# Mixing stage, first three rounds: second sums of heads split, first turn to tokens ahead of the third sums, exp table early, scaling ahead of rank

## The chip, the cores and the metric

The kernel runs on one core of a Trainium2 chip. The metric is device time in microseconds (us) of one launch; several executions are taken and their median is compared. Five engines work side by side and meet through semaphores only: PE (TensorE, matrix products and transposes), DVE (VectorE), ACT (ScalarE), POOL (GpSimd) and SP (SyncE, here only for transfers).

## The reference, cut to what matters

Two transformer layers run over 32 sequences of 256 tokens with 128 channels. The change lies in the second half of layer 1's attention and in the routing that follows it:

```python
o = o2b_weighted_delta_rule(k, q, v, b)
o = o * rsqrt(mean(o * o, axis=-1) + 1e-06) * rms_w      # per head: 16 heads of 8 channels
x = x + ga * (o.reshape(B, L, Dm) @ Wout.T + bout)
h = _layernorm(x) * (1 + cb) + sb
x = x + gb * ffn(h)
# ffn: xn = rms_norm(h); scores = xn @ w_router.T ; the 2 best of 8 experts per token,
#      weighted by softmax(scores); the expert's rows are gathered and scattered back
```

## The kernel before, in words

The program is a row of stages (load, attention, route, experts, project, delta, mix, ffn, combine). Each stage is a block with an instruction list written out by hand for each engine, and a barrier at its end. An engine works its list strictly in order, so the place of a call in the list sets what waits behind what.

The mixing stage (`mix_phase`, tiles named `mix_...`) takes the 8192 tokens in 8 rounds of 1024 tokens (two halves of 512, called `par` 0 and 1). A round i goes through these steps; the line is that of the profile before:

- `head_squares(i)` (ACT, L2518) squares the delta stage's output; `sum_heads(i)` (PE, L2405) sums the squares of each head, 8 products of which each shows as two records in the trace; `roots` (DVE, L2645 and L166 to L178) makes the reciprocal roots by Newton steps; `round_of_roots(b)` serves the heads of round b+2, the layer norm of round b and the rms norm of round b-1 in one go.
- `narrow(i)` turns the roots (PE, L2414) and copies them out (ACT, L2525); `widen(i)` (PE, L2422) spreads them over the channels; `scale_heads(i)` (DVE, L2670, tile `mix_on`) multiplies; `project_out(i)` (PE, L2428) is the product with Wout; `add_bias(i)` (ACT, L2544, tile `mix_mixed`) and `add_mixed(i)` (DVE, L2679, tensor `xT`) add it to x.
- `back(i)` (PE, L2437) turns x to tokens; `statistics(i)` (DVE, L2687, L2691) takes mean and variance; `norm(i)` (ACT, L2535) normalizes; `channels(i)` (PE, L2443) turns back; `modulate(i)` (ACT, L2554) makes h.
- `router_and_rows(i)` (PE, L2456, L2457) makes token rows and router scores; `copy_rows(i)` (ACT, L2575) copies the rows; `choose(i)` (DVE, L2709 to L2736, ends with the tile `mix_mask`) picks two experts; `exps(i)` (ACT, L2582) and `share(i)` (DVE, L2756 to L2761) make the weights; `count(i)` (PE, L2478, L2480) and `rank(i)` (DVE, L2743 to L2752, ends with `mix_place_of`) give every token its slot in its expert's list.
- `send(i)` (POOL, L2837 to L2852) copies the slots and issues 16 indirect DMAs, one for each 128 tokens and choice, which scatter the rows to the experts' lists in memory.

Every engine loops over b from -1 to 8 and handles several rounds in one pass, for instance round b+1's projection beside round b's normalization and round b-1's choice. The expert stage (`ffn`) begins when the whole block is done, the last send included. Semaphores of interest: `heads` (sums of a round ready, one count per round), `heads_read` (those sums taken by DVE), `wide`, `newton`, `mask`.

The loop of DVE around the place that is edited reads before:

```python
                if b == 1:
                    then = choose(b - 1)
                    rank(b - 1)
                    share(b - 1, then)
                if b + 1 <= LAST:
                    scale_heads(b + 1)
```

Of the kernel before, what the change touches and what calls it, by code (L numbers as in the profile page):

```python
# [180 lines left out]
PAR = 2  # L181
# [2108 lines left out]
def mix_phase(nc, dram, g):  # L2290
# [16 lines left out]
    with Scope(nc, "mix") as s:  # L2307
# [85 lines left out]

        @block.tensor
        def _(pe):
            def sum_heads(i):
                if i > 0:
                    pe.wait_ge(c.heads_read, i)
                if i > 3:
                    pe.wait_ge(c.sums_read, i - 3)  # L2400
                for par in both:
                    pe.wait_ge(k[par].sq0, i + 1)
                    for r in range(TILES):
                        first = par * TILES + r
                        last = nc.tensor.matmul(head_sums[:, first:first + 128 - SIDE + 1:SIDE], sq[:, 0, par, 128 * r:128 * r + 128],  # L2405
                                                g.t("by_head"), start=True, stop=True)
                last.then_inc(c.heads, 1)

            def narrow(i):
                pe.wait_ge(c.newton, ROOT * (i + 1))  # L2410
                if i > 0:
                    pe.wait_ge(c.narrow_out, i)
                    pe.wait_ge(k[0].mixed, i)
                nc.tensor.transpose(narrow_ps, root_y[:, i % 2, HEAD], g.t("ident")).then_inc(c.narrow, 1)  # L2414

            def widen(i):
                pe.wait_ge(c.narrow_out, i + 1)
                for par in both:
                    if i > 0:
                        pe.wait_ge(k[par].mixed, i)  # L2420
                    for r in range(TILES):
                        last = nc.tensor.matmul(mid[par][:, 128 * r:128 * r + 128], pick[:, par * TILES + r, :], inv_t[:, :],  # L2422
                                                start=True, stop=True)
                    last.then_inc(k[par].wide, 1)

            def project_out(i, par):
                pe.wait_ge(k[par].on, i + 1)
                nc.tensor.matmul(mid[par][:, :], w_out[:, :], on[:, par, :], start=True, stop=True).then_inc(k[par].out_made, 1)  # L2428

            def back(i):  # L2430
                for par in both:
                    pe.wait_ge(k[par].x_added, i + 1)
                    if i > 0:
                        pe.wait_ge(k[par].modulated, i)
                    x = g.keptT[:, cols(i, par)]
                    for r in range(TILES):
                        last = nc.tensor.transpose(front[par][:, 128 * r:128 * r + 128], x[:, 128 * r:128 * r + 128], g.t("ident"))  # L2437
                    last.then_inc(k[par].by_token, 1)

            def channels(i, par):  # L2440
                pe.wait_ge(k[par].unit, i + 1)
                for r in range(TILES):
                    last = nc.tensor.transpose(front[par][:, 128 * r:128 * r + 128], unit[:, par, r, :], g.t("ident"))  # L2443
                last.then_inc(k[par].by_channel, 1)

            def router_and_rows(i):
                if i > 0:
                    pe.wait_ge(c.counted, i)
                for par in both:
                    pe.wait_ge(k[par].modulated, i + 1)  # L2450
                    if i > 0:
                        pe.wait_ge(k[par].rows_read, i)
                    for r in range(TILES):
                        j = par * TILES + r
                        h = h4[:, par, 128 * r:128 * r + 128]
                        nc.tensor.transpose(rowt[par][:, 128 * r:128 * r + 128], h, g.t("ident"))  # L2456
                        last = nc.tensor.matmul(logits[:, j * E1:(j + 1) * E1], h, router[:, :], start=True, stop=True)  # L2457
                    last.then_inc(k[par].turned, 1)

            def sum_rows(i):  # L2460
                if i > 0:
                    pe.wait_ge(c.sums_read, i)
                for par in both:
                    pe.wait_ge(k[par].sq2, i + 1)
                    for r in range(TILES):
                        j = par * TILES + r
                        last = nc.tensor.matmul(row_sums[:, j:j + 1], sq[:, 1, par, 128 * r:128 * r + 128],
                                                g.t("ones")[:, 0:1], start=True, stop=True)
                last.then_inc(c.row_sums, 1)

            def count(i):
                pe.wait_ge(c.route, ROUTE * i + MASKED)
                if i > 0:
                    pe.wait_ge(c.placed, i)
                    pe.wait_ge(c.counted, i)
                flat = mask[:, :, :].rearrange("p j e -> p (j e)")
                WIDTH = (SIDE + 1) * E1
                nc.tensor.matmul(counts, before[:, :], flat, start=True, stop=False)  # L2478
                for d in range(1, SIDE + 1):
                    last = nc.tensor.matmul(counts[:, d * E1:WIDTH], ones[:, :], flat[:, 0:WIDTH - d * E1],  # L2480
                                            start=False, stop=d == SIDE)
                last.then_inc(c.mask, 1)

            sum_heads(0)
            sum_heads(1)
            for b in range(-1, LAST + 2):
                if b + 1 <= LAST:
                    if b == -1:
                        pe.wait_ge(c.picks, SIDE)
                    narrow(b + 1)  # L2490
                    widen(b + 1)
                if b == -1:
                    pe.wait_ge(c.w_ready, 2)
                    pe.wait_ge(c.consts, 5)
                if b == 1:
                    count(b - 1)
                for par in both:
                    if b + 1 <= LAST:
                        project_out(b + 1, par)
                    if 0 <= b <= LAST:  # L2500
                        channels(b, par)
                if b + 3 <= LAST:
                    sum_heads(b + 3)
                if b > 1:
                    count(b - 1)
                if b + 1 <= LAST:
                    back(b + 1)
                if 0 <= b <= LAST:
                    sum_rows(b)
                    router_and_rows(b)  # L2510

        @block.scalar
        def _(act):
            def head_squares(i):
                if i > 0:
                    act.wait_ge(c.heads, i)
                for par in both:
                    nc.scalar.activation(sq[:, 0, par, :], g.vT[:, cols(i, par)], ACT.Square).then_inc(k[par].sq0, 1)  # L2518
# [65 lines left out]
            def scale_up(n):  # L2584
                if n == 0:
                    act.wait_ge(c.up_in, 16)
                some = g.w_up[:, n * (2 * E1 // PIECES):(n + 1) * (2 * E1 // PIECES), :]
                nc.scalar.activation(some, some, ACT.Copy, scale=per_channel[:, 2:3]).then_inc(c.up_scaled, 1)

            head_squares(0)  # L2590
            head_squares(1)
            head_squares(2)
            act.wait_ge(c.w_in, 48)
            for b in range(-1, LAST + 2):
                if b + 1 <= LAST:
                    narrow(b + 1)
                if 0 <= b <= LAST:
                    norm(b)
                if b >= 1:
                    copy_rows(b - 1, 0)  # L2600
                if b == 1:
                    exps(b - 1)
                for par in both:
                    if b + 1 <= LAST:
                        add_bias(b + 1, par)
                    if 0 <= b <= LAST:
                        modulate(b, par)
                if 0 <= b <= LAST:
                    square(b)
                if b >= 1:  # L2610
                    copy_rows(b - 1, 1)
                if b > 1:
                    exps(b - 1)
                if 0 <= b < PIECES:
                    scale_up(b)
                if b + 4 <= LAST:
                    head_squares(b + 4)

        @block.vector
        def _(dve):  # L2620
# [169 lines left out]
            for b in range(-1, LAST + 2):  # L2790
                if b >= 0:
                    round_of_roots(b)
                if b == 1:
                    then = choose(b - 1)
                    rank(b - 1)
                    share(b - 1, then)
                if b + 1 <= LAST:
                    scale_heads(b + 1)
                if b > 1:
                    then = choose(b - 1)  # L2800
                if b + 1 <= LAST:
# [417 lines left out]
```

## Time and profile before

| what | value |
| --- | --- |
| median of 3 runs | 2004.95 us (2000.4 to 2006.43) |
| the profiled execution | 2002.02 us, span of its instructions 2000.1 us |
| busy share of the span | PE 81%, weight loads 63%, DVE 74%, ACT 59%, POOL 55% |
| granted TensorE clock, mean | 0.904 |

The shares are means over nine stages with different limits. The mixing stage is a part of the span from about 1424 us to 1655 us. A timeline row gives start, length, engine, line, operation, tiles, count, and in square brackets how long the engine sat idle before it and what released it.

### The profile page before, as it was taken

How to read it: one execution, taken by the hardware profiler on the slowest of the kernel's cores; microseconds unless marked ns; L12 is line 12 of the kernel's file. 1: busy time of each engine (PE TensorE's matmuls, PEld its weight loads, DVE VectorE, ACT ScalarE, POOL GpSimd, SP SyncE). 2: the span in 40 equal slices, each digit the busy share in tenths (PEclk: the TensorE clock that was granted, in tenths of full speed). 3: DMA queues.
4: the chain of work that ended last, by engine and by line, in shares of the span. 5: the costliest groups of instructions: out<-in, count | busy, mean ns of one | idle time of the engine just before them, and what ended most of it. 6: DMA issues, size and time to landing. Idle time of an engine off the chain costs nothing. (4 is left out here: it accounts for less than half of the span.)

```text
span 2000.1 us, 50931 instructions
## 1 busy us (share of the span) xinstructions
PE 1612.7 (81%) x17727; PEld 1252.1 (63%) x17727; DVE 1473.4 (74%) x4099; ACT 1185.8 (59%) x2762; POOL 1096.3 (55%) x1141
## 2 busy tenths in 40 slices
PE   5599999998788695698847777777789607999994
PEld 4478888887577442344325555555568607999993
DVE  8688888887499542699979999999667624555556
ACT  4566666665279721577828888887366404565551
POOL 3278888887000286233348888888437773444440
PEclk8799999999899798799969999999766658999998
DMA  4000000000501132521000000000401112222216
GB/s 120 18 3 3 4 4 4 4 3 3 219 28 41 42 45 35 147 63 43 11 0 1 1 2 1 1 1 1 185 23 48 52 60 62 66 64 65 64 51 257
DMA packets 84954, 92.34 MB, mean 46 GB/s; under 512 B 11696, under 2 KB 69296, under 8 KB 84000
## 3 DMA queue, kind: packets, MB, share of 16 engines
q1 hardware_dynamic: 67840, 62.66, 9.9%
q0 software_dynamic: 14560, 22.24, 4.3%
q10 hardware_dynamic: 2304, 4.20, 0.5%
q8 instruction: 146, 2.39, 0.5%
q14 instruction: 104, 0.85, 0.1%
HBM read 46.14 MB, written 42.91 MB: 45 GB/s over the span
## 5 line engine op out<-in xcount | busy, mean ns | idle before, releaser
L2275 POOL TENSOR_TENSOR delta_A<-delta_A,delta_sW 128x256 f32<-128x256 f32 x256 | 193.7, 757 | 79.1 <-ACT delta_sW L2122 53.0
L2045 PE MATMUL delta_u<-delta_m,tables_sb 128*128 128x256 f32 x512 | 166.7, 407 | 82.0 <-DVE delta_m L2195 82.0
L694 ACT ACTIVATE attn_p_att<-attn_score,attn_mx 128x32 f32<-128x32 f32 (+7 forms) x512 | 150.4, 409 | 134.7 <-DVE attn_mx L756 134.7
L2895 POOL DMA_INDIRECT choice_rows<-ffn_y,ffn_xg x135 | 129.7, 961 | 170.9 <-DVE ffn_y L3002 167.4
L2122 ACT ACTIVATE delta_sW<-delta_W,tables_sb 128x256 f32<-128x256 f32 x256 | 126.7, 506 | 79.9 <-DVE delta_W L2217 76.1
L2045 PEld LDWEIGHTS delta_u<-delta_m,tables_sb 128*128 128x128 f32 x512 | 87.1, 190 | 132.7 <-DVE delta_m L2195 126.0
L2041 PE MATMUL delta_u<-delta_v_own,tables_sb 128*128 128x256 f32 x512 | 153.8, 383 | 8.7 <-DVE xnT L2182 8.7
L2852 POOL DMA_INDIRECT rows<-mix_rows,mix_slot x128 | 125.5, 980 | 47.9 <-issue 38.6
L1324 POOL DMA_INDIRECT exp_rows<-rows,slot_token x32 | 33.1, 1033 | 190.4 <-SPq L142 180.9
L2217 DVE TENSOR_TENSOR delta_W<-delta_W,delta_u 128x128 f32<-128x128 f32 x512 | 133.1, 280 | 4.5
L2204 DVE TENSOR_TENSOR delta_u<-delta_u,delta_prod 128x256 f32<-128x256 f32 x256 | 109.8, 429 | 17.8 <-PE delta_u L2045 4.2
L2286 POOL TENSOR_TENSOR delta_m<-delta_A,delta_prod 128x768 f32<-128x768 f32 x64 | 122.5, 1913 | 0.0
L2994 DVE TENSOR_TENSOR ffn_hid<-ffn_sg,ffn_val 128x384 f32<-128x384 f32 x135 | 74.8, 554 | 58.7 <-PE ffn_val L2918 58.5
L2918 PE MATMUL ffn_gate<-ffn_xgT,ffn_w_up 128*128 128x128 f32 x810 | 113.8, 277 | 0.0
L2918 PE MATMUL ffn_val<-ffn_xgT,ffn_w_up 128*128 128x128 f32 x810 | 113.7, 277 | 0.0
L2113 ACT ACTIVATE delta_v_own<-delta_v_rows,tables_sb 128x256 f32<-128x256 f32 x256 | 113.4, 495 | 0.0
L2041 PEld LDWEIGHTS delta_u<-delta_v_own,tables_sb 128*128 128x128 f32 x512 | 98.3, 192 | 23.8 <-DVE xnT L2182 10.2
L756 DVE TENSOR_REDUCE attn_mx<-attn_score 128x4 f32<-128x1024 f32 (+3 forms) x128 | 98.5, 807 | 19.6 <-PE attn_score L614 18.0
L2929 PE MATMUL ffn_y<-w_down_sb,ffn_hid 128*128 x810 | 112.4, 275 | 0.0
L2195 DVE TENSOR_TENSOR delta_m<-delta_W,delta_b 128x256 f32<-128x256 f32 x256 | 106.6, 416 | 6.9 <-DVE delta_W L2217 0.5
L2958 ACT ACTIVATE ffn_w_up<-w_up_sb 128x352 f32 x135 | 67.1, 497 | 69.6 <-PEq L146 45.3
L2918 PEld LDWEIGHTS ffn_val<-ffn_xgT,ffn_w_up 128*128 128x128 f32 x810 | 102.6, 194 | 0.0
(396 smaller groups left out, 4691.4 us busy)
## 6 DMA issues: line engine op xcount, KB each, us to landing
ffn_xg<-rows SPq DMA_DIRECT2D x135, 66.0 KB, 1.8
acc<-route_zero SPq DMA_DIRECT2D x10, 832.0 KB
comb_rows<-choice_rows SPq DMA_DIRECT2D x32, 256.0 KB, 5.3
rows<-route_rows SPq DMA_DIRECT2D x8, 640.0 KB, 3.5
load_rows<-in_x SPq DMA_DIRECT2D x16, 256.0 KB, 3.8
bT<-acc SPq DMA_DIRECT2D x16, 256.0 KB, 4.1
qT<-acc SPq DMA_DIRECT2D x16, 256.0 KB, 4.7
x_kept<-xT SPq DMA_DIRECT2D x16, 256.0 KB, 2.1
```

The lines of the kernel that those rows point to most:

```text
L694: last = nc.scalar.activation(p_att[:, gr, PAIR_OFF[n]:PAIR_OFF[n] + SLOT * (n + 1)], S[:, gr, c:c + SLOT * (n + 1)], ACT.Exp, bias=mx[:, ...
L2041: nc.tensor.matmul(corrections(h, pp % 2), g.t("same_head"), moving, start=True, stop=False)
L2045: nc.tensor.matmul(corrections(h, pp % 2), g.t("same_head"), m1[:, h].rearrange("p t d b -> p (t d b)"), start=False, stop=True).then_inc( ...
L2113: ins = nc.scalar.activation(v_own[:, group % AHEAD, d], v_rows[:, group % 2], ACT.Copy, scale=g.t("less_own")[:, d:d + 1])
L2122: nc.scalar.activation(sW[:, step % RING, :], W[:, step % RING].rearrange("p d b -> p (d b)"), ACT.Copy, scale=g.t("step")[:, bass.ds(step ...
L2217: nc.vector.tensor_tensor(W[:, t % RING, :, some(h)], W[:, (t - 1) % RING, :, some(h)], changes(h, pp % 2)[:, n], ALU.subtract).then_inc(b ...
L2275: nc.gpsimd.tensor_tensor(A[:, t % 8], A[:, (t - 1) % 8], sW[:, t % RING], ALU.add).then_inc(k.A, 1)
L2286: nc.gpsimd.tensor_tensor(m3[:, t // QUAD % 2, 0:QUAD - 1], sums, query, ALU.mult).then_inc(k.m3, 1)
L2852: nc.gpsimd.indirect_dma_start(g.rows1, bass.IndirectOffsetOnAxis(slot[:, at:at + 1], 0), rows[:, i % 2, par, j, n, :], None).then_inc(sen ...
L2895: nc.gpsimd.indirect_dma_start(g.choice_rows, bass.IndirectOffsetOnAxis(xg[:, n % RING, D:D + 1].bitcast(U32), 0), y[:, n % RING, :], None ...
L2918: last = nc.tensor.matmul(out[:, 128 * p:128 * p + 128], w_up[:, n % 4, half, 128 * p:128 * p + 128], xgT[:, n % 4, :], start=True, stop=True)
L2929: last = nc.tensor.matmul(y_ps[par][:, 0:D], hid[:, n % 4, 128 * p:128 * p + 128], g.w_down[:, bass.ds(e * P + p, 1), :].rearrange("h o d ...
```

## The change

Four edits, all in the mixing stage; no arithmetic changes and no semaphore is added.

1. `sum_heads` can do one half. Round 1's sums are cut: the half `par` 0 stays ahead of the loop, the half `par` 1 (which carries the signal `heads`) moves behind `project_out(0)`.
2. `back(0)` moves from behind `sum_heads(2)` to ahead of it.
3. On ACT `head_squares(2)` moves from ahead of the loop to the end of its first pass, and one `Exp` over a column of ones takes its place, so that the exp table is loaded there.
4. On DVE, in the pass b = 1 only, `scale_heads(2)` moves ahead of `rank(0)` and `share(0)`.

```diff
-            def sum_heads(i):
+            def sum_heads(i, some=both):
...
-                for par in both:
+                for par in some:
...
-                last.then_inc(c.heads, 1)
+                if some[-1] == PAR - 1:
+                    last.then_inc(c.heads, 1)
...
             sum_heads(0)
-            sum_heads(1)
+            sum_heads(1, both[0:1])
...
+                if b == -1:
+                    sum_heads(1, both[1:2])
+                    back(0)
                 if b + 3 <= LAST:
                     sum_heads(b + 3)
                 if b > 1:
                     count(b - 1)
-                if b + 1 <= LAST:
+                if 0 <= b < LAST:
                     back(b + 1)
...
             head_squares(1)
-            head_squares(2)
+            nc.scalar.activation(ex[:, 0, 0:1], g.t("ones")[:, 0:1], ACT.Exp)
             act.wait_ge(c.w_in, 48)
...
+                if b == -1:
+                    head_squares(2)
                 if b + 4 <= LAST:
                     head_squares(b + 4)
...
+                if b + 1 <= LAST:
+                    scale_heads(b + 1)
+                if b == 1:
                     rank(b - 1)
                     share(b - 1, then)
-                if b + 1 <= LAST:
-                    scale_heads(b + 1)
```

PE at the start of the stage, before: sums of rounds 0 and 1, then round 0's turn, widening and projection, the sums of round 2, the turn to tokens (`mix_front<-tables_sb,xT`) and round 1's turn and widening.

```order
L2405 MATMUL mix_sums<-tables_sb,mix_sq 128x16 x16
L2414 MATMUL mix_mid<-tables_sb,mix_root_y 128x128
L2422 MATMUL mix_mid<-mix_inv_t,mix_pick 128x128 x8
L2428 MATMUL mix_mid<-mix_on,mix_w_out 128x512 x2
L2405 MATMUL mix_sums<-tables_sb,mix_sq 128x16 x8
L2437 MATMUL mix_front<-tables_sb,xT 128x128 x8
L2414 MATMUL mix_mid<-tables_sb,mix_root_y 128x128
L2422 MATMUL mix_mid<-mix_inv_t,mix_pick 128x128 x8
```

The same place on PE with the change:

```order
L2405 MATMUL mix_sums<-tables_sb,mix_sq 128x16 x12
L2415 MATMUL mix_mid<-tables_sb,mix_root_y 128x128
L2423 MATMUL mix_mid<-mix_inv_t,mix_pick 128x128 x8
L2429 MATMUL mix_mid<-mix_on,mix_w_out 128x512 x2
L2405 MATMUL mix_sums<-tables_sb,mix_sq 128x16 x4
L2438 MATMUL mix_front<-tables_sb,xT 128x128 x8
L2405 MATMUL mix_sums<-tables_sb,mix_sq 128x16 x8
L2415 MATMUL mix_mid<-tables_sb,mix_root_y 128x128
```

Four products of 16 stand behind the first projection now, and the turn of x to tokens stands ahead of the third sums.

DVE in the pass b = 1, from the end of `choose(0)`, before: rank (four rows), share (three rows), then the scaling of round 2 (`mix_on`).

```order
L2736 TENSOR_TENSOR mix_mask<-mix_onehot 128x64
L2743 TENSOR_TENSOR mix_place<-mix_small,mix_base 128x64
L2746 TENSOR_TENSOR mix_base<-mix_base,mix_small 128x8
L2747 TENSOR_TENSOR mix_own<-mix_onehot,mix_place 128x128
L2752 TENSOR_REDUCE mix_place_of<-mix_own 128x16
L2756 TENSOR_REDUCE mix_total<-mix_ex 128x8
L2757 RECIPROCAL mix_total<-mix_total 128x8
L2761 TENSOR_TENSOR mix_rows<-mix_ex,mix_total 128x16
L2670 TENSOR_TENSOR mix_on<-mix_mid,xnT 128x512 x2
L2679 SCALAR_TENSOR_TENSOR xT<-mix_mixed,mod,xT 128x256 x4
```

The same place on DVE with the change:

```order
L2742 TENSOR_TENSOR mix_mask<-mix_onehot 128x64
L2676 TENSOR_TENSOR mix_on<-mix_mid,xnT 128x512 x2
L2749 TENSOR_TENSOR mix_place<-mix_small,mix_base 128x64
L2752 TENSOR_TENSOR mix_base<-mix_base,mix_small 128x8
L2753 TENSOR_TENSOR mix_own<-mix_onehot,mix_place 128x128
L2758 TENSOR_REDUCE mix_place_of<-mix_own 128x16
L2762 TENSOR_REDUCE mix_total<-mix_ex 128x8
L2763 RECIPROCAL mix_total<-mix_total 128x8
L2767 TENSOR_TENSOR mix_rows<-mix_ex,mix_total 128x16
L2685 SCALAR_TENSOR_TENSOR xT<-mix_mixed,mod,xT 128x256 x4
```

The two rows that scale round 2 moved from the end to right behind the mask.

## Rows read from the trace of the kernel before

**Rows 1.** Instructions of line L2852, the sends: ns min/median/max, first and last start.

```profile
L2852 POOL DMA_INDIRECT rows<-mix_rows,mix_slot x128: 953/960/1558, 1474.8 to 1652.9; - x128
```

**Rows 2.** Timeline of POOL: batches 0, 1 and 2 of the sends.

```profile
1474.83 1.08 POOL L2852 DMA_INDIRECT rows<-mix_rows,mix_slot  x1 [2.43 <-DVE mix_rows L2761]
...
1500.60 0.20 POOL L2840 CAST mix_slot<-mix_place_of 128x16 uint32<-128x16 f32 x1 [5.23 <-DVE mix_place_of L2752]
1502.42 0.98 POOL L2852 DMA_INDIRECT rows<-mix_rows,mix_slot  x1 [1.63 <-issue]
...
1524.24 0.97 POOL L2852 DMA_INDIRECT rows<-mix_rows,mix_slot  x1 [0.77 <-issue]
```

**Rows 3.** Timeline of PE, first three rounds.

```profile
1429.18 3.56 PE L2405 MATMUL mix_sums<-tables_sb,mix_sq 128*128 128x16 f32 x16 [0.81 <-ACT mix_sq L2518]
...
1434.15 3.79 PE L2422 MATMUL mix_mid<-mix_inv_t,mix_pick 128*128 128x128 f32 x16 [1.11 <-ACT mix_inv_t L2525]
1437.72 2.89 PE L2428 MATMUL mix_mid<-mix_on,mix_w_out 128*128 128x512 f32 x4
1442.51 3.02 PE L2405 MATMUL mix_sums<-tables_sb,mix_sq 128*128 128x16 f32 x16 [1.89 <-DVE mix_root_v L2645]
1445.37 1.95 PE L2437 MATMUL mix_front<-tables_sb,xT 128*128 128x128 f32 x8
...
1447.90 3.04 PE L2422 MATMUL mix_mid<-mix_inv_t,mix_pick 128*128 128x128 f32 x16 [0.37 <-ACT mix_inv_t L2525]
1452.99 1.70 PE L2428 MATMUL mix_mid<-mix_on,mix_w_out 128*128 128x512 f32 x2 [2.06 <-DVE mix_on L2670]
...
1457.38 1.86 PE L2405 MATMUL mix_sums<-tables_sb,mix_sq 128*128 128x16 f32 x16
...
1465.12 3.78 PE L2422 MATMUL mix_mid<-mix_inv_t,mix_pick 128*128 128x128 f32 x16 [0.37 <-ACT mix_inv_t L2525]
...
1474.62 2.08 PE L2428 MATMUL mix_mid<-mix_on,mix_w_out 128*128 128x512 f32 x2 [3.46 <-DVE mix_on L2670]
```

**Rows 4.** Timeline of ACT, first three rounds.

```profile
1428.41 1.15 ACT L2518 ACTIVATE mix_sq<-xnT 128x512 f32<-128x512 f32 x2 [3.16 <-PE mix_sums L2405]
1432.78 1.15 ACT L2518 ACTIVATE mix_sq<-xnT 128x512 f32<-128x512 f32 x2 [3.23 <-PE mix_sums L2405]
...
1471.56 1.28 ACT L2582 ACT_TABLE_LOAD   x1
1472.86 0.27 ACT L2582 ACTIVATE mix_ex<-mix_less 128x80 f32<-128x80 f32 x1
1476.73 0.69 ACT L2544 ACTIVATE mix_mixed<-mix_mid,mix_per_channel 128x512 f32<-128x512 f32 x1 [3.60 <-PE mix_mid L2428]
```

**Rows 5.** Timeline of DVE, first three rounds.

```profile
1431.04 0.29 DVE L178 SCALAR_TENSOR_TENSOR mix_root_y<-mix_root_t,mix_root_y 128x128 f32<-128x128 f32 x1
...
1440.48 1.78 DVE L2679 SCALAR_TENSOR_TENSOR xT<-mix_mixed,mod,xT 128x256 f32<-128x256 f32 x4 [1.81 <-ACT mix_mixed L2544]
...
1446.57 1.68 DVE L2687 BATCH_NORM_STATS2 mix_stats<-mix_front 128x6 f32<-128x128 f32 x8 [1.57 <-PE mix_front L2437]
...
1452.25 1.28 DVE L2670 TENSOR_TENSOR mix_on<-mix_mid,xnT 128x512 f32<-128x512 f32 x2
...
1470.38 0.22 DVE L2736 TENSOR_TENSOR mix_mask<-mix_onehot 128x64 bf16<-128x64 f32 x1
...
1473.16 0.22 DVE L2756 TENSOR_REDUCE mix_total<-mix_ex 128x8 f32<-128x64 f32 x1 [1.02 <-ACT mix_ex L2582]
...
1473.87 1.29 DVE L2670 TENSOR_TENSOR mix_on<-mix_mid,xnT 128x512 f32<-128x512 f32 x2
```

**Rows 6.** Busy time by stretch: PE, weight loads, DVE, ACT, POOL; granted clock, DMA.

```profile
1424.00:1439.80 15.80, 13.10 (x52) 11.62 (x53) 4.99 (x18) 3.73 (x8) 6.13 (x14) 0.50 0.90 359
...
1456.80:1463.70 6.90, 6.90 (x66) 6.76 (x65) 4.84 (x24) 5.03 (x8) 0.00 (x0) 0.99 0.01 4
1463.70:1480.70 17.00, 11.42 (x49) 8.46 (x47) 10.45 (x40) 9.14 (x21) 4.84 (x6) 0.50 0.05 16
```

## The prediction

> **What bounds the kernel now.** The page gives no single bound, since nine stages share the span, so I read only the stage that is edited, engine by engine in time. The first question there is which engine finishes last. The instructions of the send line come first [rows 1]: POOL issues 128 scattering transfers between 1474.8 and 1652.9 us, and the expert stage starts only when they are done. The timeline of POOL [rows 2] then shows how tightly they are packed. Batch 1 starts at 1502.42 and batch 2 at 1524.24, so 16 sends with what lies between two batches take 21.82. From batch 1's first send to the last send of all, 1652.9 - 1502.4 = 150.5 pass; six such periods (130.9) and the 15 steps inside the last batch (15/16 of a period at most, 20.5) give 151. So from batch 1 on POOL never waits for anything that matters, and whatever else gets faster there is worth nothing. Ahead of it POOL does wait: 1502.42 - 1474.83 = 27.59, that is 5.77 over a period, and the row of the slots names the wait, 5.23 for the ranks of round 1. The end of the stage therefore moves by what **batch 1's first send** moves, and by no more than the first send of batch 0 moves plus 5.77.
>
> The work that leads to that send is a chain over PE, ACT and DVE [rows 3 to 5]. It has three places where the chain stands still because of list order: the sums of round 1 ahead of round 0's turn, the sums of round 2 ahead of the turn to tokens, and the scaling of round 2 behind rank and share. The edits lie on these three.
>
> **Edit 1 and the ACT part of edit 3: start of round 0.** The roots of round 0 end at 1431.04 + 0.29 = 1431.33 [rows 5]. PE could turn them then, but is in the 16 records of round 1's sums from 1429.18 to 1432.74, and ACT, which must copy the turned roots, is in round 2's squares until 1432.78 + 1.15 = 1433.93. The widening starts at 1434.15 [rows 3, 4]. With half the sums left, PE is free at 1429.18 + 3.56/2 = 1430.96. ACT is free once the early exp is done: squares until 1428.41 + 1.15 = 1429.56, table load 1.28, one exp, below the 0.27 of the 80-column one: 1431.1. Both are in time for 1431.33. What remains is the turn and the copy. From below they take what the copy and its signals took behind the squares, 1434.15 - 1433.93 = 0.22; from above 1434.15 - 1432.74 = 1.41, from the end of the sums with ACT's delay inside. A turn is one product of the kind whose eight take 1.95, so I take 0.25 plus filling, and 0.3 for the copy with two signals, in all about 1.1: widening at 1432.4, a gain of 1.75 (bounds 1.4 to 2.6).
>
> The table load was hidden nowhere before (DVE idles 1.02 for the exp [rows 5]); now its cover is PE's half sums and the roots. Without that cover it would cost ACT up to 1431.1 - 1429.56 = 1.5 us at this place. The exp row starts at 1472.86, and the load ends at 1471.56 + 1.28 = 1472.84 [rows 4]: a load costs 1.28 and nothing behind it. The Trainium skill, page "ScalarE: Activation LUTs", section "What ACT_TABLE_LOAD costs", gives a drain of about 1380 ns on top of 1283 ns for each switch of the set. By it ACT would be free only at 1432.5, later than the turned roots, and this gain would be about 0.4 us smaller; the trace shows the 1283 ns and no drain, so I leave it out.
>
> **Edits 1 and 2: round 0's turn to tokens.** Projection of round 0 starts 1.75 earlier and ends at 1437.72 + 2.89 - 1.75 = 1438.9; if its second half, which ran behind 1439.8, gets the half clock, 0.7 later. The second half of round 1's sums, 1.8 at half clock, fills a gap in which PE waited 1.89 for DVE's roots before [rows 3]: it ends at 1440.6 to 1441.3. DVE ends adding to x at 1442.26 - 1.75 = 1440.5 (to 1441.2), and then makes the roots of round 1, which now need that second half. They took from 1442.26 to 1446.57 - 1.57 = 1445.0, so 2.8: now done at 1443.5 to 1444.2. What is late next is the turn to tokens: eight transposes of 1.95 in all start at 1440.6 to 1441.3, so the first half is there by 1442.3, before DVE needs it. So the statistics start at 1443.5 to 1444.2 instead of 1446.57, a gain of 2.4 to 3.1; with the same 5.68 behind it as before (1446.57 to 1452.25), DVE could scale round 1 at 1449.2 to 1449.9.
>
> The price is on PE and ACT: the sums of round 2 now stand behind the turn. They start at 1442.6 to 1443.2 and take 1.86 to 3.56 (full or half clock, [rows 3]): 1444.5 to 1446.8. ACT's squares of round 3 wait for that (1.15), then comes the copy for round 1: widening from 1445.9 to 1448.1 with 3.04 to 3.79: ends 1449.0 to 1451.9. Round 1's projection needs that and the scaled half: it starts between 1450.0 and 1451.7 instead of 1452.99. Gain 1.3 to 3.0; I take **2.2**, the middle, since clock there changed within the stretch before.
>
> **Edit 4: scaling ahead of rank.** `choose(0)` ends at 1470.38 + 0.22 = 1470.60; scaling began at 1473.87 [rows 5]. Nothing else holds it: the widening of round 2 ended at 1465.12 + 3.78 = 1468.90 [rows 3]. So the scaling moves 3.27 ahead of the rest of its round, and it is what both others wait for: PE idles 3.46 for it, ACT 3.60 for the projection behind it [rows 3, 4]. What moves back is rank and share, 1.29 later; but share had 1.02 of waiting for the exp with its table load, which is gone, and rank waited for the counts of PE in that time too. So batch 0's first send stays within 0.3 of where edits 1 and 2 put it, and it has room: it is batch 1 that decides. I take **3.2** for batch 1.
>
> Sum: 2.2 + 3.2 = 5.4 for batch 1's first send: 1497.0. POOL could start it one period after batch 0's first send: 1474.83 - 2.2 + 21.8 = 1494.4. So POOL still waits some 2.6 there, and the whole 5.4 reaches the end. By the bounds: 1.3 + 3.2 = 4.5 to 3.0 + 3.2 = 6.2; the limit set by POOL is 2.2 + 5.77 = 8.0.
>
> **The rivals.**
> - *The clock rises later.* The stretch from round 3's sums to the router runs at the full clock before (0.99 over 6.9 us), and the next 17 us at half [rows 6]. The same 16 records take 3.56 at half and 1.86 at full clock, so 6.9 us at full would be 13 at half. If half of the stretch falls to half clock by its new place in time, 3.1 is lost: gain 2.3. If all falls, the gain is about zero.
> - *The clock rises sooner.* PE loses two waits, 1.89 and 3.46. If this brings the full clock sooner, up to the POOL limit of 8.0 is won. For it speaks that the 17 us at half clock held PE busy only 11.42; against it that 13.10 busy of 15.80 at the stage's start were at half clock throughout [rows 6]. The Trainium skill, page "TensorE: Matmul & The Clock Gate", Part 1, says that half rate is the default and that PE's activity releases it; by that rule this case is the likelier one, and the trace agrees only in part.
> - *The chain is not what feeds batch 1.* If something outside the three places holds the ranks of round 1, the end does not move: 0 to 2 us.
> - *Slower.* Scaling now stands ahead of rank and waits for the widening of round 2, with 1470.60 - 1468.90 = 1.7 to spare. Were the widening later than that relative to `choose`, batch 0's first send would slip one for one. It decides the end only when that send comes after 1502.42 - 21.82 = 1480.6, so widening would have to be 7.5 late; for 0.3% slower some 13.5. Both hang on the same PE, whose router stands just ahead of it, so I hold little of it.
>
> **How the numbers follow.** The four executions shown run from 2000.4 to 2006.43, so 0.3%, 6 us, is about what a measurement can tell from no change. Against the profiled execution the sum gives 2002.02 - 5.4 = 1996.6, against the median 2004.95 - 5.4 = 1999.6; the mean of the four executions, 2003.45, lies between, and I predict 2003.45 - 5.4 = **1998.0**. Chances: forecast (4.5 to 6.2) 0.5; clock later, 2001, 0.2; clock sooner, 1995.5, 0.2; no effect, 2003, 0.06; slower, 2012, 0.04. The range runs from 2002.02 - 8.0 = 1994.0 to 2006.43 - 2.3 = 2004. Faster by over 0.3% means under 1998.9 against the median: the sooner clock, and three fifths of the forecast, whose gain lies just at that mark: 0.2 + 0.3 = 0.5. Within 0.3%: 0.46. Slower: 0.04.
>
> **What would show it.** Right: widening of round 0 about 1.7 after the end of half the sums; statistics of round 0 some 2.4 to 3.1 earlier; no PE wait of 3.46 ahead of round 2's projection; first sends of batch 0 about 2 and of batch 1 about 5.4 earlier, and after that the same period of 21.8 to the end. Wrong: a first send of batch 1 that moves by another amount with PE's granted clock changed in the stretch ahead of it; a wait in POOL that returns in batch 2 or later, when the rows or ranks of round 2 don't keep up; or an expert stage of another length.

## The result, and the profile after

The changed kernel takes 1992.57 us (median of 6 runs, 1991.28 to 1993.35) against 2003.07 us before (2000.4 to 2006.43, 6 runs): ratio 0.9947, 95% interval 0.9934 to 0.996, so 8 to 13 us less. Timed twice more, the ratio was 0.9955 (0.9941 to 0.9968) and 0.9943 (0.9929 to 0.9956). The forecast was 1998.0 with a range of 1994.0 to 2004.0: the direction is right, the gain is about twice the 5.4 us that were forecast, and the time lies below the range.

The profiled execution of the changed kernel took 1991.99 us, its span is 1990.0. The sends, to be set beside [rows 1]:

```profile
L2859 POOL DMA_INDIRECT rows<-mix_rows,mix_slot x128: 952/958/1556, 1468.1 to 1643.5; - x128
```

The timeline of POOL, batches 0, 1 and 2 [rows 2]:

```profile
1468.08 1.08 POOL L2859 DMA_INDIRECT rows<-mix_rows,mix_slot  x1 [1.31 <-DVE mix_rows L2767]
...
1491.15 0.20 POOL L2847 CAST mix_slot<-mix_place_of 128x16 uint32<-128x16 f32 x1 [2.58 <-DVE mix_place_of L2758]
1492.74 0.97 POOL L2859 DMA_INDIRECT rows<-mix_rows,mix_slot  x1 [1.39 <-issue]
...
1514.54 0.97 POOL L2859 DMA_INDIRECT rows<-mix_rows,mix_slot  x1 [0.77 <-issue]
```

Batches 1 and 2 still lie 21.80 apart (21.82 before), and from batch 1 to the last send pass 150.8 us (150.5 before): POOL is the bound as it was. Its first sends came 6.75 and 9.68 sooner. Of both, 1.67 is not the change: PE's first sums of the stage began at 1423.11 and not at 1424.78, and nothing ahead of them differs. Counted from the first sums, as in everything that follows, batch 0 is 5.1 sooner (45.0 for 50.05) and batch 1 is 8.0 sooner (69.6 for 77.6).

The timeline of PE at the start of the stage [rows 3]:

```profile
1423.11 3.60 PE L2405 MATMUL mix_sums<-tables_sb,mix_sq 128*128 128x16 f32 x16 [1.98 <-ACT mix_sq L2522]
1427.51 1.86 PE L2405 MATMUL mix_sums<-tables_sb,mix_sq 128*128 128x16 f32 x8 [0.81 <-ACT mix_sq L2522]
1429.80 0.45 PE L2415 MATMUL mix_mid<-tables_sb,mix_root_y 128*128 128x128 f32 x1 [0.42 <-DVE mix_root_y L178]
1430.68 3.31 PE L2423 MATMUL mix_mid<-mix_inv_t,mix_pick 128*128 128x128 f32 x16 [0.43 <-ACT mix_inv_t L2529]
1433.82 2.07 PE L2429 MATMUL mix_mid<-mix_on,mix_w_out 128*128 128x512 f32 x4
1435.73 0.96 PE L2405 MATMUL mix_sums<-tables_sb,mix_sq 128*128 128x16 f32 x8
...
1438.08 1.86 PE L2405 MATMUL mix_sums<-tables_sb,mix_sq 128*128 128x16 f32 x16
...
1441.34 3.79 PE L2423 MATMUL mix_mid<-mix_inv_t,mix_pick 128*128 128x128 f32 x16 [0.54 <-ACT mix_inv_t L2529]
1446.74 2.08 PE L2429 MATMUL mix_mid<-mix_on,mix_w_out 128*128 128x512 f32 x2 [1.61 <-DVE mix_on L2676]
...
1465.10 2.07 PE L2429 MATMUL mix_mid<-mix_on,mix_w_out 128*128 128x512 f32 x2
```

The second half of round 1's sums takes 0.96 where the first took 1.86; the sums of round 2 take 1.86 where they took 3.02 before; round 0's projection takes 2.07 and not 2.89. These are durations at full clock, as the second window below shows for the stretch that they lie in. The wait of 3.46 ahead of round 2's projection is gone, and ahead of round 1's PE waits 1.61 for DVE: PE was not what held round 1. The windows say the same (columns as in [rows 6]):

```profile
1423.10:1433.10 10.00, 8.33 (x36) 7.88 (x37) 3.30 (x12) 3.38 (x6) 5.48 (x13) 0.50 0.88 336
1433.10:1440.10 7.00, 6.53 (x43) 4.94 (x41) 5.13 (x15) 2.65 (x5) 0.00 (x0) 0.98 1.01 437
1440.10:1450.60 10.50, 8.12 (x25) 5.79 (x26) 7.54 (x32) 5.56 (x14) 0.00 (x0) 0.51 0.76 272
```

Full clock (the 2.4 GHz level) is granted from 10 us after the first sums for 7 us; before it came at 15 us [rows 6] and lasted 3.4 us, as the row of the kernel before for that stretch shows:

```profile
1439.80:1443.20 3.40, 1.51 (x8) 0.69 (x7) 2.60 (x8) 1.25 (x2) 0.00 (x0) 0.99 0.98 424
```

The timelines of ACT and DVE [rows 4, 5]:

```profile
1427.90 1.28 ACT L2596 ACT_TABLE_LOAD   x1
1429.20 0.20 ACT L2596 ACTIVATE mix_ex<-tables_sb 128x1 f32<-128x1 f32 x1
1430.35 0.28 ACT L2529 ACTIVATE mix_inv_t<-mix_mid 128x128 f32<-128x128 f32 x1 [0.95 <-PE mix_mid L2415]
```

```profile
1429.36 0.29 DVE L178 SCALAR_TENSOR_TENSOR mix_root_y<-mix_root_t,mix_root_y 128x128 f32<-128x128 f32 x1
...
1435.68 1.85 DVE L2685 SCALAR_TENSOR_TENSOR xT<-mix_mixed,mod,xT 128x256 f32<-128x256 f32 x4 [0.97 <-ACT mix_mixed L2548]
...
1440.31 1.68 DVE L2693 BATCH_NORM_STATS2 mix_stats<-mix_front 128x6 f32<-128x128 f32 x8
...
1446.00 1.28 DVE L2676 TENSOR_TENSOR mix_on<-mix_mid,xnT 128x512 f32<-128x512 f32 x2
...
1464.23 0.22 DVE L2742 TENSOR_TENSOR mix_mask<-mix_onehot 128x64 bf16<-128x64 f32 x1
1464.36 1.28 DVE L2676 TENSOR_TENSOR mix_on<-mix_mid,xnT 128x512 f32<-128x512 f32 x2
```

The early exp ends at 1429.40, just before the roots at 1429.65, and ACT then waits 0.95 for PE: the load is fully covered. DVE makes round 0's statistics without any wait, and the scaling of round 2 follows the mask at once.

### The profile page after: what moved, and what is told of

It reads as the page before. It is cut to its first block and busy times, and to the rows that moved or that the text cites. A ratio compares the mean times of both kernels' runs of the same rounds, so it can differ in the third digit from the quotient of the medians.

```text
span 1990.0 us, 50933 instructions
## 1 busy us (share of the span) xinstructions
PE 1607.8 (81%) x17727; PEld 1249.7 (63%) x17727; DVE 1472.8 (74%) x4099; ACT 1184.9 (60%) x2763; POOL 1094.5 (55%) x1141
## 5 line engine op out<-in xcount | busy, mean ns | idle before, releaser
L2859 POOL DMA_INDIRECT rows<-mix_rows,mix_slot x128 | 125.3, 979 | 46.8 <-issue 38.7
```

The source lines that it names most:

```text
L2859: nc.gpsimd.indirect_dma_start(g.rows1, bass.IndirectOffsetOnAxis(slot[:, at:at + 1], 0), rows[:, i % 2, par, j, n, :], None).then_inc(sen ...
```

## The experiments

**Theory.** The list order frees three waits, as forecast; with that, TensorE's clock rises sooner, which shortens PE's work in round 0 and at times in round 2. **Rivals.** The waits alone (then the clock of the first profile is luck); a gain outside the stage; a gain from one of the edits alone.

The table gives what the profiles show, all in us from PE's first sums of the stage (that start itself in the second column, from the span's start). The third column is the first rise to full clock after the first sums, read from windows of half a us.

| profile | first sums | full clock | statistics 0 | first send, batch 0 | batch 1 | last send |
| --- | --- | --- | --- | --- | --- | --- |
| before | 1424.78 | 15.0 | 21.8 | 50.05 | 77.6 | 228.1 |
| before_2 | 1427.01 | 15.0 | 21.8 | 50.05 | 77.6 | 230.0 |
| before_3 | 1423.50 | 14.0 | 21.8 | 49.7 | 77.0 | 226.8 |
| before_4 | 1425.11 | 15.0 | 21.8 | 50.1 | 77.7 | 229.5 |
| after | 1423.11 | 10.0 | 17.2 | 45.0 | 69.6 | 220.4 |
| after_again | 1425.54 | 11.5 | 17.7 | 45.55 | 67.3 | 216.8 |
| after_3 | 1426.59 | 12.0 | 17.9 | 44.0 | 66.0 | 217.5 |
| only_scale | 1425.43 | 15.0 | 21.8 | 50.1 | 72.0 | 223.9 |
| no_scale | 1425.73 | 11.5 | 17.7 | 45.2 | 71.5 | 222.1 |
| no_turn | 1425.31 | 11.5 | 17.7 | 45.6 | 67.3 | 217.7 |
| no_split | 1426.26 | 11.5 | 18.4 | 46.2 | 70.9 | 221.3 |
| no_exp | 1424.05 | 12.0 | 17.9 | 44.7 | 66.2 | 217.0 |
| squares_late | 1425.17 | 12.0 | 18.6 | 46.8 | 74.4 | 224.9 |
| squares_late_2 | 1426.87 | 11.5 | 18.4 | 46.6 | 74.1 | 225.0 |
| squares_late_3 | 1424.89 | 12.0 | 18.6 | 46.8 | 74.45 | 226.0 |
| squares_and_scale | 1426.33 | 11.5 | 18.5 | 46.8 | 68.6 | 218.2 |
| choose_early | 1424.07 | 11.0 | 17.5 | 45.4 | 66.9 | 217.0 |
| busy_best | 1426.96 | 10.0 | 17.0 | 44.1 | 65.5 | 215.8 |
| busy_before | 1426.22 | 14.0 | 21.6 | 49.6 | 76.8 | 228.0 |

**Scaling alone (only_scale) and all but scaling (no_scale).**

```diff
                 if b == 1:
                     then = choose(b - 1)
+                if b + 1 <= LAST:
+                    scale_heads(b + 1)
+                if b == 1:
                     rank(b - 1)
                     share(b - 1, then)
-                if b + 1 <= LAST:
-                    scale_heads(b + 1)
```

> The kernel before with edit 4 alone: the scaling of round 2 ahead of rank and share of round 0. Both theories (waits of list order alone; the same plus a TensorE clock that rises sooner in round 0) expect the first send of batch 0 within 0.5 us of the kernel before, counted from the stage's first sums, and the first send of batch 1 some 3.2 us sooner, with 3.2 us less in all (ratio 0.998). If the 10.5 us of the whole change lay in scaling, this run would give over 6.

> The changed kernel without edit 4 (scaling back behind rank and share). Waits alone: first sends of batches 0 and 1 both about 2.2 us sooner than before, 2.2 us less in all. With the clock: both about 4.6 us sooner, full clock in round 0's projection and turn to tokens, 4.6 us less in all.

Scaling alone: ratio 0.9981 (0.9966 to 0.9996), 0.19% of 2001.59, so 3.8 us. Batch 0 does not move; batch 1 moves by 5.6, more than the 3.3 of the move. PE's granted clock rose at 49 us and not at 56 there, which is the likely source of the rest. It was 21.9 behind batch 0, so POOL's wait was gone:

```profile
1496.14 0.23 POOL L2838 COPY mix_rows<-mix_ids 128x16 uint32<-128x16 uint32 x1
1496.29 0.20 POOL L2841 CAST mix_slot<-mix_place_of 128x16 uint32<-128x16 f32 x1
1497.40 0.97 POOL L2853 DMA_INDIRECT rows<-mix_rows,mix_slot  x1 [0.91 <-POOL mix_slot L2841]
```

Without scaling: ratio 0.9969 (0.9957 to 0.9981), 6.2 us; statistics of round 0 4.1 sooner, batch 0 4.8 sooner, and the wait for ranks stays:

```profile
1495.77 0.20 POOL L2846 CAST mix_slot<-mix_place_of 128x16 uint32<-128x16 f32 x1 [3.70 <-DVE mix_place_of L2758]
```

So edits 1 to 3 give 4.8 at the first send, not 2.2. The two parts add up, 3.8 + 6.2 = 10.0 beside the 9 to 11.4 of the whole in its three timings, though each part is known only within 2.4 to 3 us.

**Without the early turn (no_turn).**

```diff
                 if b == -1:
                     sum_heads(1, both[1:2])
-                    back(0)
...
-                if 0 <= b < LAST:
+                if b + 1 <= LAST:
                     back(b + 1)
```

> The changed kernel without edit 2: the first turn to tokens again behind the sums of round 2. Waits alone: the turn is late by one set of sums, 1.9 us at full clock to 3.6 at half, so statistics of round 0 start 1 to 2 us later than in the changed kernel (its roots of round 1 cover the rest), and 1 to 2 us of its gain are lost. With the clock as the larger part: nearly all of the gain stays if the full clock in round 0 stays, since round 0's widening and projection are where it rises.

Ratio 0.9954 (0.9936 to 0.9972), 9.2 us: no loss shows. The sums of round 2 take 1.96 at full clock and end while DVE is still in the roots of round 1, so the turn is not late even behind them, and the statistics have no wait:

```profile
1440.48 1.96 PE L2405 MATMUL mix_sums<-tables_sb,mix_sq 128*128 128x16 f32 x16 [1.10 <-DVE mix_root_v L2650]
```

```profile
1442.67 0.29 DVE L178 SCALAR_TENSOR_TENSOR mix_root_y<-mix_root_t,mix_root_y 128x128 f32<-128x128 f32 x1
1443.03 1.68 DVE L2692 BATCH_NORM_STATS2 mix_stats<-mix_front 128x6 f32<-128x128 f32 x8
```

Edit 2 is worth nothing that shows.

**Without the split (no_split).**

```diff
-            sum_heads(1, both[0:1])
+            sum_heads(1)
...
                 if b == -1:
-                    sum_heads(1, both[1:2])
                     back(0)
```

> The changed kernel with the sums of round 1 whole ahead of the loop. Waits alone: widening of round 0 starts 1.1 to 1.8 us later than in the changed kernel, and as much of the gain is lost. With the clock: the clock rises in round 0's projection as in the kernel before, one step later, and 3 us or more are lost, with round 0's turn to tokens partly at half clock.

Ratio 0.9975 (0.9963 to 0.9987), 5.0 us, so half of the gain is lost in the times. The profile shows widening at 8.70 and not 7.58, 1.1 later, and the first sends 0.7 and 3.6 later than in after_again; the clock rose at the same 11.5. The expected loss of clock in round 0 did not happen. The larger loss lies behind batch 0: POOL waits 2.44 for the ranks of round 1, and PE got full clock only at 49 us, where it came at 42.0 in no_turn and 42.5 in after_again. Beside no_turn, timed against the same runs of the kernel before, the medians differ by 1996.50 - 1992.74 = 3.8 us and batch 1's first sends by 70.9 - 67.3 = 3.6.

**Squares alone (squares_late), three profiles, two timings.**

```diff
             head_squares(1)
-            head_squares(2)
...
+                if b == -1:
+                    head_squares(2)
                 if b + 4 <= LAST:
                     head_squares(b + 4)
```

> The kernel before with a single move: the squares of round 2 on ACT from ahead of the loop to the end of its first pass, so that the copy of round 0's roots no longer waits for them. Waits alone: widening of round 0 starts 0.7 us sooner and batch 0's first send with it, 0.7 us in all. With the clock: full clock rises at about 11.5 us after the first sums and not 15, round 0's statistics start some 3 us sooner, and both first sends move by 3 us or more.

> The single move of squares, a second profile. If its pattern is one, batch 0's first send is again at 46.8 us and batch 1's at 74.4. If it has two patterns, one of them is near the kernel before, 49 to 50 and 77.

> The single move of squares, timed again. If what the profiles show reaches the end, the ratio to the kernel before is 0.9983 (3.3 us less); if something behind the stage's sends gives it back, the ratio is 0.9995 or more as in the first timing.

PE's timeline in the first of them:

```profile
1425.17 3.60 PE L2405 MATMUL mix_sums<-tables_sb,mix_sq 128*128 128x16 f32 x16 [1.98 <-ACT mix_sq L2518]
1429.58 3.57 PE L2405 MATMUL mix_sums<-tables_sb,mix_sq 128*128 128x16 f32 x16 [0.81 <-ACT mix_sq L2518]
...
1433.88 3.51 PE L2422 MATMUL mix_mid<-mix_inv_t,mix_pick 128*128 128x128 f32 x16 [0.43 <-ACT mix_inv_t L2525]
1437.22 2.07 PE L2428 MATMUL mix_mid<-mix_on,mix_w_out 128*128 128x512 f32 x4
1441.19 1.96 PE L2405 MATMUL mix_sums<-tables_sb,mix_sq 128*128 128x16 f32 x16 [1.90 <-DVE mix_root_v L2646]
1443.00 1.21 PE L2437 MATMUL mix_front<-tables_sb,xT 128*128 128x128 f32 x8
```

PE's order here is that of before. The widening starts only 0.66 sooner (8.71 for 9.37), but projection, the sums of round 2 and the turn take 2.07, 1.96 and 1.21 instead of 2.89, 3.02 and 1.95 [rows 3], and statistics start 3.2 sooner, again without a wait. The windows, with PE's clock as the third number from the end, then the row of the statistics:

```profile
1425.20:1436.70 11.50, 10.26 (x46) 9.88 (x47) 3.69 (x12) 1.87 (x4) 5.46 (x13) 0.50 0.94 365
1436.70:1443.70 7.00, 5.10 (x32) 3.53 (x32) 4.93 (x14) 2.92 (x5) 0.00 (x0) 0.98 0.97 418
```

```profile
1443.74 1.68 DVE L2688 BATCH_NORM_STATS2 mix_stats<-mix_front 128x6 f32<-128x128 f32 x8
```

With PE's order as it was, 0.66 of the 3.2 is the wait that went; the other 2.5 comes from PE's shorter times at full clock. All three profiles of this kernel show it (batch 0 at 46.6 to 46.8, batch 1 at 74.1 to 74.5). The times show less: 0.9995 (0.9986 to 1.0005) and 0.9997 (0.9982 to 1.0013), so 0.6 to 1.0 us where 3.3 were expected. The interval of the first timing allows at most 2.8 us, that of the second 3.6. Part of the gap lies in the recorded executions of the kernel before: the four of them average 2002.7 us, above the medians of 1999.77 and 2000.51 of its executions in these two timings, while the three of the kernel with the squares moved average 1999.6, beside its medians of 1999.05 and 1999.27. Where in the program the recorded executions of the kernel before were longer than usual is open.

**Squares and scaling (squares_and_scale).** The edits of only_scale and squares_late together.

> The kernel before with two moves only: squares of round 2 on ACT to the end of the first pass, and scaling of round 2 ahead of rank and share. By the sum of the single runs (3.2 us on both batches from the squares, 3.2 to 5.7 on batch 1 from the scaling): batch 0's first send at 46.8 us after the first sums, batch 1's at 68.6 to 71, 6.5 to 9 us less in all. If the split of the sums and the early turn carry the gain instead, under 5.

Ratio 0.9969 (0.9954 to 0.9983), 6.2 us; the profile has 46.8 and 68.6, as the sum of the single moves said. The time is just under the 6.5 to 9 that were expected. What this pair lacks beside the changed kernel is the split with its 1.1 us of widening, the early turn and the early exp.

**Without the early exp (no_exp).**

```diff
-            nc.scalar.activation(ex[:, 0, 0:1], g.t("ones")[:, 0:1], ACT.Exp)
```

> The changed kernel without the early exp. The table load of 1.28 us stands again ahead of the exp of round 0. Both theories: batch 0's first send some 0.5 to 1 us later than in the changed kernel, batch 1's unchanged if it waits for ranks, so no more than 1 us in all.

One execution of 1990.42. Between the slots and batch 0's first send POOL waits 1.92 for the shares where it waited 1.31, so the load costs 0.6 there; batch 0 still came 0.3 sooner than in the first profile of the changed kernel. The clock was full from 22.5 to 32.5 us here, which is the likely reason. The exp is worth less than the spread among the profiles.

**The changed kernel again (after_again, after_3) and the kernel before (before_2, before_3, before_4).**

> The changed kernel once more, beside the others on this chip. If the larger gain came from a clock that rises sooner because of the order (theory), full clock comes again within 10 to 12 us of the stage's first sums, batch 0's first send again about 5 us sooner than before, and the median again 8 to 11 us under before. If the first profile was luck of the clock (rival), the rise falls at 15 us as before, batch 0's first send is only 2 to 3 us sooner and the gain near 5.4.

> The changed kernel, timed beside it on the same chip: ratio 0.995 as twice before, and first sends of batches 0 and 1 within 45 to 46 and 67 to 70 us after the first sums.

> The kernel before, a second profile. If its clock pattern belongs to the order (theory), full clock rises again 15 us after the stage's first sums, the first sends of batches 0 and 1 come again at about 50.0 and 77.6 us and the last at 228. If it was one of several patterns (rival: the place of the clock's changes against the stage varies from execution to execution), the times differ by 2 us or more and the first profile was one of the longer ones, which would explain why the single move of squares won 3.2 us against that profile and 0.7 us in the medians.

> The kernel before, a third profile, as the second: first sends at 50.0 and 77.6 us if the pattern belongs to the order; another pair, 2 us or more away, if it varies.

> The kernel before, a fourth profile, as the second and third: with all four the range of batch 0's and batch 1's first sends is known, to be compared with 45.0 and 69.6 us and 45.6 and 67.3 us of the two profiles of the changed kernel.

The pattern of round 0 belongs to the order. In the six profiles with the squares in the old place (four of before, only_scale, busy_before) the rise came at 14 to 15 us and full clock lasted 3.4 us; in the thirteen with the squares moved it came at 10 to 12 us and lasted 6.8 to 6.9. So it then covers the projection, the sums of round 2 and the turn. The clock's last fall ahead of the stage does not repeat as well: read in windows of 0.1 us, it came 1.6 to 2.3 us ahead of the first sums in 14 profiles. In four of them the squares stand in the old place, and the rise came 17.1 us after the fall; in the other ten they are moved, and it came 13.6 to 13.7 after it. The fall in before and in after_again (columns as in [rows 6], the clock is the third number from the end):

```profile
1422.28:1422.78 0.50, 0.50 (x16) 0.25 (x12) 0.00 (x0) 0.00 (x0) 0.00 (x0) 0.90 0.00 0
1422.78:1423.28 0.50, 0.02 (x3) 0.00 (x0) 0.00 (x0) 0.39 (x1) 0.00 (x0) 0.50 0.00 0
```

```profile
1423.04:1423.54 0.50, 0.50 (x16) 0.25 (x12) 0.00 (x0) 0.00 (x0) 0.00 (x0) 1.00 0.00 0
1423.54:1424.04 0.50, 0.02 (x3) 0.00 (x0) 0.00 (x0) 0.38 (x1) 0.00 (x0) 0.50 0.00 0
```

In the other five profiles the fall came 3.3 to 6.8 us ahead of the first sums. The first profile of the changed kernel is one of them: its fall lies 6.8 ahead and its rise 17.0 behind the fall, so the place of its rise at 10 is in part chance.

The first sends of before lie within 0.4 and 0.7 us of each other. Those of the changed kernel lie at 44.0 to 45.6 and 66.0 to 69.6, so batch 1 is 7.4 to 11.7 sooner, and at batch 1 the first profile was the poorest of the three. Batch 1's spread comes from the second place: in the first profile full clock covered only 48 to 51 us of the stretch between the batches, in after_again 42.5 to 49, and there batch 1 followed batch 0 at 21.8 with no wait. Outside this part little changed: the first sums lie at 1423.50 to 1427.01 in before and at 1423.11 to 1426.59 in the changed kernel, from batch 1's first send to the last send pass 149.8 to 152.4 and 149.4 to 151.5 us, and from the last send to the end of the span 346.7 to 347.5 and 345.6 to 347.0. The means of the three differ by 0.0, 0.5 and 0.8 us, which leaves little to the rival of a gain elsewhere. What follows batch 1's first send varies by some 3 us by itself.

**Early choice in pass b = 2 (choose_early) and idle products (busy_best, busy_before).** The first is the changed kernel with the order of pass b = 1 used in pass b = 2 too, on PE, ACT and DVE; DVE's part is shown:

```diff
+    EARLY = 2
...
-                if b == 1:
+                if 1 <= b <= EARLY:
                     then = choose(b - 1)
                 if b + 1 <= LAST:
                     scale_heads(b + 1)
-                if b == 1:
+                if 1 <= b <= EARLY:
                     rank(b - 1)
                     share(b - 1, then)
...
```

> The changed kernel with the order that pass b = 1 has on choice, count, exp, rank and share used in pass b = 2 as well: choice of round 1 ahead of the scaling of round 3. If batch 1's first send is what sets the end, POOL's wait ahead of it (2.58 us in the profile of the changed kernel) is gone, batch 1 starts 21.8 us behind batch 0, and the time is 2 to 3 us under the changed kernel. If the end is set by batch 0 alone, nothing moves. Scaling of round 3 is some 3.5 us later, which batch 2 must bear: if it doesn't, a wait appears ahead of batch 2.

The wait of POOL is gone (batch 1 21.5 behind batch 0, no bracket ahead of the slots), but the ratio is 0.9955 (0.9941 to 0.9968), that of after_again beside it. In that kernel the wait had mostly gone by itself, so the expected 2 to 3 us were a price from the poorest profile.

```profile
1489.83 0.23 POOL L2845 COPY mix_rows<-mix_ids 128x16 uint32<-128x16 uint32 x1
1489.97 0.20 POOL L2848 CAST mix_slot<-mix_place_of 128x16 uint32<-128x16 f32 x1
1490.94 0.98 POOL L2860 DMA_INDIRECT rows<-mix_rows,mix_slot  x1 [0.77 <-issue]
```

busy_best is choose_early with idle products on PE (products whose result nothing reads); busy_before has the first of these lines alone, in the kernel before:

```diff
+            keep_busy(rowt[0][:, 0:128], 4)
             sum_heads(0)
...
+                if b == 1:
+                    pe.wait_ge(c.heads_read, b + 3)
+                    pe.wait_ge(c.sums_read, b)
+                    keep_busy(sums[:, 128:256], 3)
...
+                if b == 0:
+                    keep_busy(rowt[0][:, 0:128], 3)
```

> The changed kernel with the early choice in pass b = 2 and idle products on PE where it waits: 4 ahead of the first sums, 3 ahead of round 1's projection, 3 ahead of round 0's counts; they write a part of PSUM that nothing reads. With the clock as a cause: full clock in more of the first 50 us, batch 0's first send at 43 to 44 us instead of 45.3, 1 to 2 us less than the changed kernel. If only order counts: no gain, or up to 1 us lost where the products run into the work.

> The kernel before with 4 idle products on PE ahead of the first sums, where PE waits 2 us for the first squares; no order changes. With the clock as a cause: if full clock comes sooner than 15 us after the first sums, round 0's statistics start sooner by 1 to 3 us. If only order counts, or the clock does not rise: 21.8 us as in all four profiles of the kernel before.

busy_best has the earliest first send of batch 1, 65.5, and one of the earliest of batch 0, 44.1 (44.0 in after_3). Full clock came at 10.0 and again at 23.5 to 30.5 and 40.5 to 47.5, but the first rise was 13.6 us after the last fall ahead of the stage, no sooner than without idle products, and the ratio of 0.9947 (0.9933 to 0.9961) is that of the changed kernel. No version beat the changed kernel beyond the interval. busy_before had its rise at 14.0 as before_3, 17.1 us after the last fall, so the four products did not bring it forward. The rise came 1 us sooner than in three of the four profiles of before, but round 0's statistics only 0.2 sooner (21.6), where the expectation named 1 to 3 for such a case: full clock was over at 17.2 us, and the sums of round 2, which began at 17.1, took 3.49. So a sooner rise by itself was worth little; what counted was the work that fell into the stretch at full clock. As the idle products moved no clock, the run doesn't test the theory.

## Why the prediction was right and wrong

- **The bound: right.** POOL's sends end the stage, batch 1's first send sets them, and no wait for ranks comes back behind it. The wait of 2.6 that the forecast left ahead of batch 1 is met by the first profile (2.58) by luck: both sends had moved by more than forecast, and in the other two profiles the wait is gone.
- **Edit 1 and ACT's squares, widening of round 0: right.** Forecast 1.75 (1.4 to 2.6), measured 9.37 - 7.57 = 1.8. The sign that the forecast named, widening 1.7 after the end of half the sums, does not fit its own sum (1432.4 - 1430.96 = 1.44); measured are 1430.68 - 1429.37 = 1.31. The drain at a table load that the Trainium skill gives (page "ScalarE: Activation LUTs", section "What ACT_TABLE_LOAD costs") is not seen here either: 1427.90 + 1.28 = 1429.18, and the exp starts at 1429.20.
- **"Edits 1 and 2: round 0's turn to tokens", the gain of 2.2: this step failed.** It kept PE's clock where it was before in time (rise at 15 us): the projection kept its 2.89 or took 0.7 longer, the second half of the sums took 1.8 at half clock, the sums of round 2 took 1.86 to 3.56 behind the turn, and PE's widening of round 1 was the limit for its projection. The runs showed a rise at 10 to 12 us, and a full clock that lasted twice as long, in every kernel with the squares moved. Round 0's addition to x then ended 3.1 sooner, not 1.75: 1.8 from the widening's start and 1.25 from widening and projection, 5.21 us from start to end for 6.46. The statistics, which had waited 1.57 for the turn, followed the roots of round 1 with no wait, 4.6 sooner (4.1 and 3.9 in the other two profiles) where 2.4 to 3.1 were forecast. The widening of round 1 ended at 1445.13, ahead of DVE's scaling at 1446.00, and round 1's projection, whose start the 2.2 priced, came 4.6 sooner (23.6 us after the first sums for 28.2; 4.1 and 3.9 in the other two). All of it reached batch 0: 4.5 to 6.0 for 2.2, against the first profile of before. Scaling left out, the times give 6.2 for it.
- **The price of the new place of round 2's sums: wrong.** The sums were put at up to half clock, which let the widening of round 1 end 24.2 to 27.1 us after the first sums; at full clock they took 1.86 and it ended at 22.0. The early turn that this price was to buy is worth nothing that shows (no_turn).
- **Edit 4: right, with more behind it.** The move itself is 3.4 (from the start of the mask to the scaling 0.13 us for 3.49), beside 3.2 in the forecast; alone it gave 3.8 us. In some profiles PE, which no longer idles 3.46, gets full clock sooner there and batch 1 gains 2 to 3 more.
- **The rivals and the range.** "The clock rises sooner" came true and was given 0.2. Its limit of 8.0 was built on the failing term (2.2 + 5.77); with 4.5 to 6.0 for batch 0 the limit is 10.3 to 11.8, which the measured 9 to 11.4 nearly fills. The low end of 1994.0 stood on that 8.0. The forecast gave the clock a chance but took its most likely course as unchanged, where the change brought forward just the PE work, widening and projection of round 0, behind which the clock had risen before.
- **Open:** why the clock's pattern changed as it did; by how much the squares' move reaches the times (3.3 in profiles, 0.6 to 1.0 in times), so the clock's part of the gain is shown in the profiles and not sized in the times; and whether the late full clock that delayed batch 1 without the split (no_split) belongs to that order or to its one profile.

## What to carry to other kernels

Find the one transfer or instruction that starts the bound engine's unbroken run, and price an edit by how much sooner that one starts; what gets faster behind it is hidden. Where an edit removes PE waits in a stretch at half clock, price the stretch at both clocks and build the limit of the gain from the best case of every term, not from the likeliest. One profile of each kernel isn't enough below 1%: here the start of the stage alone moved by 3.5 us between executions, so times should be counted from a mark in the stage.

## What the runs showed of the hardware

- PE was at half clock for 15.8 us at the start of the stage while its records filled 13.10 of them [rows 6]. In every profile of the table full clock came only when the widening of round 0 had begun or was over, never during the two sets of sums ahead of it.
- The moves of the clock repeat with the program: in four profiles of before the first rise fell at 14.0 to 15.0 us after the first sums, though the stage began anywhere from 1423.50 to 1427.01. With a widening that starts 0.66 sooner it came at 11.5 to 12.0, and full clock lasted 6.8 us and not 3.4.
- A table load took 1.28 us in a stretch with transfers of 336 GB/s on average, as in a quiet one with 16 GB/s [rows 4, 6].
